# Expert blocks of 128 rows instead of 256, four to a slot, in batch groups of 5, 5, 4 and 2, with the sums at one pace

## The reference

```
x = layernorm(x + attention(x))          16 heads of 16 channels, rope, causal
x = layernorm(x + experts(x))

experts: probs = softmax(x @ gate_w.T)   32 experts
         top 8 of 32 per token, their weights made to sum to 1
         out = sum over the 8 experts e of
               w_e * ((u * silu(g)) @ down_w[e].T),   g, u = split(x @ gate_up_w[e].T)
```

## Time and profile before

| what | us |
|---|---|
| time of 3 runs: median (lowest, highest) | 2408.0 (2407.4, 2415.5) |
| span of the profiled execution | 2400.9 |
| between that span and the median (work around the span; the profiled execution's time is not listed apart) | 7.1 |
| PE busy | 2019.5 (84%) |
| DVE busy | 1642.8 (68%) |
| ACT busy | 1559.1 (65%) |
| POOL busy | 1124.8 (47%) |
| DMA engines, mean busy share, q1 (SP's queue) and q0 (POOL's) | 51.1% and 19.6% |

### The profile page before, as it was taken

How to read it: one execution, slowest core, us unless ns; L and a number is a source line. 1 busy time by engine, 2 the same in 40 slices (tenths; PEclk the granted TensorE clock), 3 DMA queues, 4 the chain that set the end, 5 groups by cost and what they waited for, 6 DMA issues and landing times.

```text
span 2400.9 us, 57843 instructions
## 1 busy us (share of the span) xinstructions
PE 2019.5 (84%) x18031; PEld 1445.3 (60%) x18031; DVE 1642.8 (68%) x3500; ACT 1559.1 (65%) x3163; POOL 1124.8 (47%) x1110
## 2 busy tenths in 40 slices
PE   4888888888888888888788899999899999998970
PEld 2444444454445444444446788788788788787760
DVE  4777777777776677777654555555577777777774
ACT  1566665666655555555456677777688788888870
POOL 1004345534553355544455005000677777777776
PEclk8899999999999899999999999999999999999995
DMA  5455667657766866557957669788999999999993
GB/s 169 129 168 187 190 213 241 199 181 218 247 209 200 281 217 221 183 173 229 318 174 256 213 205 342 254 270 279 316 353 333 317 339 322 327 336 320 318 302 116
DMA packets 330818, 591.91 MB, mean 247 GB/s; under 512 B 47168, under 2 KB 168416, under 8 KB 328416
## 3 DMA queue, kind: packets, MB, share of 16 engines
q1 hardware_dynamic: 251232, 400.17, 51.1%
q0 software_dynamic: 53760, 159.45, 19.6%
q10 hardware_dynamic: 25536, 28.58, 3.6%
HBM read 326.68 MB, written 299.50 MB: 261 GB/s over the span
## 4 chain that ended last, share of the span: by engine, by line
PE 37%; DMA 15%; DVE 15%; issue 11%; ACT 8%; POOL 6%; SPq 5%; ACTq 2%; DVEq 1%; POOLq 0%
POOL stacks L759 4%; DMA qk_parts<-pbuf 4%; DVE mn L1484 4%; PE ps L935 4%; PE ps L1008 4%; PE ps L989 3%; PE ps L876 3%; PE ps L991 3%; PE ps L990 3%; PE ps L923 3%; ACT work L1143 3%; PE ps L901 3%; SPq L591 2%; PE ps L825 2%; DMA stacks<-qk_parts 2%
## 5 line engine op out<-in xcount | busy, mean ns | idle before, releaser
L1143 ACT ACTIVATE pT<-ps 128x1024 f16<-128x1024 f16 (+4 forms) x1408 | 827.8, 601 | 428.6 <-PE ps L925 277.7
L743 POOL DMA_INDIRECT x_sorted<-xhl,idx x512 | 532.8, 1041 | 414.9 <-DVE xhl L1555 263.4
L759 POOL DMA_INDIRECT stacks<-y_sorted,idx x512 | 520.1, 1016 | 362.0 <-DMA y_sorted<-work 199.9
L1484 DVE TENSOR_REDUCE mn<-ps 128x1 f32<-128x512 f32 (+3 forms) x704 | 416.4, 633 | 93.7 <-PE ps L903 89.3
L989 PE MATMUL ps<-pT,gu_hi 128*128 128x256 f16 x1536 | 421.5, 274 | 18.4 <-issue 12.7
L990 PE MATMUL ps<-pT,gu_hi 128*128 128x256 f16 x1536 | 421.0, 274 | 0.0
L991 PE MATMUL ps<-pT,gu_lo 128*128 128x256 f16 x1536 | 420.8, 274 | 0.0
L923 PE MATMUL ps<-stacks 99*128 99x512 bf16 (+3 forms) x1024 | 310.7, 317 | 65.6 <-ACT pT L1143 44.7
L901 PE MATMUL ps<-stacks 96*128 96x512 bf16 (+3 forms) x1024 | 293.1, 319 | 58.7 <-DMA stacks<-qk_parts 31.6
L1051 PE MATMUL ps<-dn,vx 128*128 x768 | 210.1, 274 | 31.3 <-DVE work L1661 16.1
L1647 DVE TENSOR_TENSOR vx<-vx 128x512 f16<-128x512 f32 x192 | 132.4, 690 | 151.6 <-ACT vx L1143 137.2
(11 more groups left out here) (229 smaller groups left out, 3621.3 us busy)
## 6 DMA issues: line engine op xcount, KB each, us to landing
y_sorted<-work SPq DMA_DIRECT2D x288, 256.0 KB
stacks<-qk_parts SPq DMA_DIRECT2D x128, 384.0 KB, 5.1
x_sorted<-zeros_h SPq DMA_DIRECT2D x132, 288.0 KB
stacks<-x_sorted SPq DMA_DIRECT2D x88, 288.0 KB, 4.4
y_sorted<-yev SPq DMA_DIRECT2D x96, 256.0 KB
qk_parts<-pbuf SPq DMA_DIRECT2D x62, 384.0 KB
pT<-x_sorted SPq DMA_DIRECT2D x70, 288.0 KB
pbuf<-x_sorted SPq DMA_DIRECT2D x70, 288.0 KB
```

Source lines behind the costliest of these rows:

```text
L743: pool.indirect_dma_start(xsort[g][:, :], bass.IndirectOffsetOnAxis(ap=at, axis=0), xhl_rows[:, t, :], None).then_inc(s_scat, 16)
L759: pool.indirect_dma_start(yg[:, r, k, :].bitcast(I32), None, ysort[g][:, :], bass.IndirectOffsetOnAxis(ap=at, axis=0)).then_inc(s_yg[r], 16)
L1143: return nc.scalar.activation(o, i, f, **k)
L1484: V.tensor_reduce(mn[:, tt, h0:h0 + nh], ps[:, odd_bank("max", at, m), 0:nh * n].rearrange("p (a n) -> p a n", a=nh), axis=AX.X, op=ALU.ma ...
```

## The change

`BLK` becomes 128, and a slot holds four blocks, each with its own expert; what was a block of 256 rows is now a pair (`PAIR`), whose two halves are loaded, multiplied and stored apart. The worst case of blocks is (tokens x 8 / 128 + 32) per group, in slots of four 48 + 48 + 40 + 24 = 160. Groups are 5, 5, 4 and 2 batches. The register tables take 16 numbers at a time. The plan of sums gives a tile every 2.1 slots (`TILE_PACE` 21) once its group is ready: total 0 at slot 56, 47 totals (0 to 46) below slot 160, and 17 behind it. `bias` gives up its memory to share `rcb`'s, and the homes of the later part are taken in another order.

```diff
@@ -64,31 +64,29 @@
-BLK = 256
-GROUPS = ((0, 7), (7, 12), (12, 15), (15, 16))
+BLK, PAIR = 128, 256
+GROUPS = ((0, 5), (5, 10), (10, 14), (14, 16))
 NG = len(GROUPS)
...
 MB = GMAX * T // BLK
-NSLOT = [((hi - lo) * T * TOPK // BLK + E) // 2 for lo, hi in GROUPS]
+NSLOT = [((hi - lo) * T * TOPK // BLK + E) // 4 for lo, hi in GROUPS]
 SLOT0 = [sum(NSLOT[:g]) for g in range(NG + 1)]
...
 RW = 2 * C + 2 * E
-TILES = [(SLOT0[g + 1] + 8, SLOT0[g + 2] + 7) for g in range(NG - 1)] + [(S + 8, S + 12)]
-NK = TILES[-1][1]
 NXT = 4
...
 NYG = 3
-NREG = 8
+NREG, NTAIL = 16, 8
 RT = 11
...
 WT = 4
-TPARTS = [-(-2 * n // P) for n in NSLOT]
+TPARTS = [-(-4 * n // P) for n in NSLOT]
 TB = [0]
...
@@ -96,18 +94,21 @@
-    tiles_at = {}
-    for (lo, hi), (first, last) in zip(GROUPS, TILES):
-        tiles = list(range(lo * NT, hi * NT))
-        for k, q in enumerate(tiles):
-            tiles_at.setdefault(first + k * (last - first) // len(tiles), []).append(q)
+    tiles_at, at = {}, 0
+    for g, (lo, hi) in enumerate(GROUPS):
+        at = max(at, 10 * (SLOT0[g + 1] + 8))
+        for q in range(lo * NT, hi * NT):
+            tiles_at.setdefault(at // 10, []).append(q)
+            at += TILE_PACE
     return tiles_at
...
+TILE_PACE = 21
 TILES_AT = plan()
+FIRST_SUM, NK = min(TILES_AT), max(TILES_AT) + 1
 LATER = 2 * (SLOT0[1] - 12)
-EARLY_HOMES, LATE_HOMES = list(range(14)), list(range(10, 20))
+EARLY_HOMES, LATE_HOMES = list(range(14)), list(range(14, 20)) + list(range(10, 14))
 HOMES = [EARLY_HOMES[n % 14] if n < LATER else LATE_HOMES[(n - LATER) % 10] for n in range(2 * S)]
...
@@ -133,7 +134,7 @@
 def y_on_vector(n):
-    return n % 2 == 1 and n // 2 + LAG < TILES[0][0]
+    return n % 2 == 1 and n // 2 + LAG < FIRST_SUM
...
@@ -477,10 +478,10 @@
-                g = GROUP_OF[n // 2]
-                n -= (n - 2 * SLOT0[g]) % NREG
-                j = n - 2 * SLOT0[g]
-                count = min(NREG, 2 * NSLOT[g] - j)
+                g = GROUP_OF[n // 4]
+                n -= (n - 4 * SLOT0[g]) % NREG
+                j = n - 4 * SLOT0[g]
+                count = min(NREG, 4 * NSLOT[g] - j)
                 if j == 0:
...
@@ -593,15 +594,15 @@
             y_row = Table(sp, 2, [n - BLK for n in NROW])
-            tail_regs = [sp.alloc_register(f"tail_{k}") for k in range(NREG)]
+            tail_regs = [sp.alloc_register(f"tail_{k}") for k in range(NTAIL)]
...
                     wait(sp, s_tab, g + 1)
-                if e % NREG == 0:
-                    sp.load(tail_regs, ztab[0:1, g, e:e + NREG])
-                row = sp.snap(tail_regs[e % NREG], min_val=0, max_val=NROW[g] - BLK)
+                if e % NTAIL == 0:
+                    sp.load(tail_regs, ztab[0:1, g, e:e + NTAIL])
+                row = sp.snap(tail_regs[e % NTAIL], min_val=0, max_val=NROW[g] - BLK)
                 sp.dma_start(xsort[g][bass.ds(row, BLK), :].rearrange("(a b) c -> a (b c)", a=16),
...
@@ -625,14 +626,15 @@
                     wait(sp, s_yc[k % NYR], 2 * (k // NYR + 1))
-                src = xsort[g][bass.ds(x_row(n), BLK), :].rearrange("(p m) c -> p m c", m=2)
-                sp.dma_start(xrows[HOMES[n]], src).then_inc(s_xs[HOMES[n]], 16)
+                for m in range(2):
+                    sp.dma_start(xrows[HOMES[n]][:, m, :], xsort[g][bass.ds(x_row(2 * n + m), BLK), :]).then_inc(s_xs[HOMES[n]], 16)
...
                 wait(sp, s_yc[n % NYR], 2 * (n // NYR + 1))
-                dst = ysort[GROUP_OF[n // 2]][bass.ds(y_row(n), BLK), :].rearrange("(p m) c -> p m c", m=2)
-                sp.dma_start(dst, ysb[n % NYR].bitcast(I32)).then_inc(s_ys[n % NYR], 16)
+                for m in range(2):
+                    dst = ysort[GROUP_OF[n // 2]][bass.ds(y_row(2 * n + m), BLK), :]
+                    sp.dma_start(dst, ysb[n % NYR][:, m, :].bitcast(I32)).then_inc(s_ys[n % NYR], 16)
...
@@ -752,7 +754,7 @@
                     for k in range(NYR):
-                        wait(pool, s_ys[k], 16 * (2 * SLOT0[g + 1] // NYR))
+                        wait(pool, s_ys[k], 32 * (2 * SLOT0[g + 1] // NYR))
                 wait(pool, s_cmb, 7 * (q - NYG) + 3)
...
@@ -998,14 +1000,14 @@
                 k = BANK_X[n % 2]
-                wait(pe, s_xs[HOMES[n]], 16 * (len(uses_before(n)) + 1))
+                wait(pe, s_xs[HOMES[n]], 32 * (len(uses_before(n)) + 1))
                 if n < 2:
...
                     for m in range(2):
-                        last = nc.tensor.transpose(o[:, c * BLK + m * P:c * BLK + (m + 1) * P],
+                        last = nc.tensor.transpose(o[:, c * PAIR + m * P:c * PAIR + (m + 1) * P],
                                                    xnat[HOMES[n]][:, m, c * P:(c + 1) * P], identh[:, :])
...
@@ -1021,21 +1023,23 @@
                     n = 2 * s + a
-                    e, r = expert(n), n % NXT
+                    r = n % NXT
                     if m == 0:
                         wait(pe, s_xe, n + 1)
-
-                    def weights(w, kc):
-                        return w[:, bass.ds(e, 1), kc, m, :].rearrange("p o f -> p (o f)")
-                    last = hilo(ps[:, k, a * BLK:(a + 1) * BLK],
-                                [weights(gu_hi, kc) for kc in range(NC)], [weights(gu_lo, kc) for kc in range(NC)],
-                                [xT[:, r, kc, :] for kc in range(NC)], [xT[:, r, NC + kc, :] for kc in range(NC)])
+                    for b in range(2):
+                        e, rows = expert(2 * n + b), slice(b * BLK, (b + 1) * BLK)
+
+                        def weights(w, kc):
+                            return w[:, bass.ds(e, 1), kc, m, :].rearrange("p o f -> p (o f)")
+                        last = hilo(ps[:, k, a * PAIR + b * BLK:a * PAIR + (b + 1) * BLK],
+                                    [weights(gu_hi, kc) for kc in range(NC)], [weights(gu_lo, kc) for kc in range(NC)],
+                                    [xT[:, r, kc, rows] for kc in range(NC)], [xT[:, r, NC + kc, rows] for kc in range(NC)])
                 last.then_inc(done, 1)
...
                 n, r = 2 * s + a, s % 2
-                e, k = expert(n), y_bank(n)
+                k = y_bank(n)
                 wait(pe, s_h, s + 1)
...
@@ -1044,10 +1048,11 @@
                     wait(pe, s_yc[last_in_bank % NYR], 2 * (last_in_bank // NYR + 1))
-                d_hi, d_lo = (dn[:, bass.ds(e, 1), p, :].rearrange("p o c -> p (o c)") for p in range(2))
                 for m in range(2):
+                    e = expert(2 * n + m)
+                    d_hi, d_lo = (dn[:, bass.ds(e, 1), p, :].rearrange("p o c -> p (o c)") for p in range(2))
                     o = ps[:, k, m * C:(m + 1) * C]
-                    h_hi, h_lo = (h[:, r, a * BLK + m * P:a * BLK + (m + 1) * P] for h in (hh, hl))
+                    h_hi, h_lo = (h[:, r, a * PAIR + m * P:a * PAIR + (m + 1) * P] for h in (hh, hl))
                     mmul(o, h_hi, d_hi, start=True, stop=False)
...
@@ -1274,9 +1279,9 @@
                 wait(act, s_h, s - 1)
-                for a in range(2):
+                for a in range(4):
                     actv(hf[:, s % 2, a * BLK:(a + 1) * BLK], ps[:, BANK_G[s % 2], a * BLK:(a + 1) * BLK], ACT.Tanh,
-                         scale=mgh[:, bass.ds(expert(2 * s + a), 1)]).then_inc(s_th, 1)
+                         scale=mgh[:, bass.ds(expert(4 * s + a), 1)]).then_inc(s_th, 1)
...
@@ -1291,10 +1296,10 @@
                 else:
-                    wait(act, s_ys[n % NYR], 16 * (n // NYR))
+                    wait(act, s_ys[n % NYR], 32 * (n // NYR))
                 for m in range(2):
                     actv(ysb[n % NYR][:, m, :], ps[:, y_bank(n), m * C:(m + 1) * C], ACT.Copy,
-                         scale=xw[HOMES[n]][:, m, bass.ds(expert(n), 1)]).then_inc(s_yc[n % NYR], 1)
+                         scale=xw[HOMES[n]][:, m, bass.ds(expert(2 * n + m), 1)]).then_inc(s_yc[n % NYR], 1)
```

More of the change, by code:

```diff
@@ L252, in build @@
         bvc = sb("bvc", [P, NC])
-        bias = sb("bias", [P, C])
         ident = sb("ident", [P, P])
@@ L267, in build @@
         rcb = sb("rcb", [P, C])
+        bias = rcb
         mhalf = sb("mhalf", [P, NT])
@@ L310, in build @@
         ind = lg2[:, 1, :]
-        tab = sb("tab", [3, 2 * S], I32)
+        tab = sb("tab", [3, 4 * S], I32)
         ztab = sb("ztab", [1, NG, E], I32)
@@ L1597, in table_out @@
                 wait(dve, s_ttr, g + 1)
-                V.tensor_copy(tab[:, 2 * SLOT0[g]:2 * SLOT0[g + 1]], ps[0:3, odd_bank("table", GROUPS[g][1]), 0:2 * NSLOT[g]]).then_inc(s_tab, 1)
+                V.tensor_copy(tab[:, 4 * SLOT0[g]:4 * SLOT0[g + 1]], ps[0:3, odd_bank("table", GROUPS[g][1]), 0:4 * NSLOT[g]]).then_inc(s_tab, 1)
             def ln_add(b, v):
@@ L1631, in gated @@
             def gated(s):
-                wait(dve, s_th, 2 * s + 2)
+                wait(dve, s_th, 4 * s + 4)
                 V.scalar_tensor_tensor(out=hf[:, s % 2, :], in0=hf[:, s % 2, :], scalar=1.0, in1=ps[:, BANK_G[s % 2], :],
@@ L1658, in rows_copy @@
                 else:
```

(4 more changed lines are left out.)

## The result

The changed kernel takes 2539.0 us (median of 4 runs, 2538.3 to 2546.5), the kernel before beside it 2407.7: ratio **1.0579** (95% interval 1.0548 to 1.0610), 131 us slower. The forecast was 2388, its range ended at 2450. The profiled span is 2536.5 us, 135.6 longer than before.

The account below looks back on a forecast made before the run. PE's register instructions were to set the pace: 5.24 + 0.37 table load + 0.27 waits = 5.88 us a slot; 1282.5 + 159 x 5.88 + 163 = 2380 us span, plus 7.1 gives 2388 us, range 2330 to 2450.

Parts of the forecast that it names:

- The bound moves to instructions, not columns: PE in a slot: register and other sequencer instructions, 5.24 us, exceed the array's 4.90 and set the pace.
- rival D: PE's array: 128-column matmuls that load their own weights take over 0.056 us; time 2480, chance 0.05.
- PE's floor of 5.61: PE per slot: 5.24 us of sequencer instructions plus 0.37 for its table load.
- SP at 5.3 a slot: SP: eight issues of 0.525 us, table loads and the sums' transfers take 5.3 us a slot, hidden behind PE's 5.6.
- rival C: SP issues in order, so transfers come late and PE waits each slot; 6.27 us a slot, time 2450, chance 0.31.
- The excess: 0.27 kept of 0.63: Waits per slot beyond the array's 4.83 us were 0.63; 0.27 of it was taken to stay above PE's new floor.
- Table loads as a term of PE alone: PE's load of 16 numbers every fourth slot adds 0.37 us a slot; ACT's and SP's loads stay below PE's floor.
- The sequencer is ahead, which now it never is: PE's sequencer, as the bound, never runs ahead, so short waits aren't caught up; all 0.63 us a slot could stay.
- the first of the two signs of being wrong: PE's gate_or_up matmuls going on 0.056 us apart over several groups while register instructions keep their spacing would refute the forecast.
- The end: After the last slot, 17 tiles instead of 7 remain: 163 us against 76.8 before.
- Attention at 0: Register tables built at other batches during attention: cost put at 0, between -5 and +5 us.
- Rival B: PE's register instructions run beside the array's queue at no new cost; slot stays 5.45 us, time 2319, chance 0.12.

Follow-up runs that it names:

- e9: The changed kernel with PE taking a fixed expert's weights, so no register instructions or table load on PE; 2470.7 us, ratio 1.0295.
- e5: The changed kernel with gate and up in matmuls of 256 columns, both blocks of a pair using the first block's expert; 2491.5 us, ratio 1.0372.
- e7: The changed kernel with each pair loaded from fixed sorted rows by one SP transfer (the fixed load); 2486.0 us, ratio 1.0372.
- e8: The changed kernel with pairs loaded from fixed rows by one transfer and gate and up in matmuls of 256 columns; 2409.9 us, ratio 1.0040.
- e6: The changed kernel with ACT and DVE loading their table numbers only once, using other experts' scales; 2502.3 us, ratio 1.0428.
- e14: The changed kernel with 256-column gate and up, one fixed-row transfer per pair, and table loads ahead of the waits; 2352.8 us, ratio 0.9811.
- g1: The kernel before with table loads issued ahead of the waits, results unchanged; 2386.5 us, ratio 0.9947.

## Why the prediction was wrong, point by point

- **The bound moves to instructions, not columns: right in direction.** Eight transposes take 0.45, gate products are 0.056 apart where they aren't starved; rival D is out. But PE's sequencer was not the only one that it moved to.
- **PE's floor of 5.61: a little low.** The instructions came as counted (44.6 for 44.8 a slot), 0.118 each where nothing stops them (gate groups 0.237 apart from 2139.36 to 2140.07). The table load, every fourth slot, has a median of 1.25, a mean of 1.37 in 1900 to 2200 us and 0.36 behind it, so about 0.43 a slot for 0.37. That gives 5.7 (the 5.9 in the expectations above takes 0.12 and 0.48). This is the smaller part.
- **SP at 5.3 a slot, "hidden behind 5.6": wrong, and the step that failed.** The 0.525 of the earlier trace rows is the distance of issues that all take 0.34 to 0.36 us. Among the sums an issue takes 0.43 on average, 29 of 404 in 300 us over 0.6, and with what stands around it a transfer costs 0.64; 8.8 of them (the sums' included) are 5.6, and table loads make it 6.1. So SP's floor is above PE's, and it is the one that stands when PE's register work is taken away (e9, 6.2 to 6.4). It was to be had before: 275 issues took 112.6 us there, 0.41 each, and SP was taken for 3.4 of 5.45 us a slot, not "under half". With 6.1, rival C would have been the likeliest case.
- **The excess: 0.27 kept of 0.63, wrong in kind.** I treated the waits as one amount laid on top of one floor. In fact PE (5.7) and SP (6.1) are both nearly full and the measured excess over the higher floor is 0.6 (0.4 in 1950 to 2250 us). That each waits for the other by way of ACT, and neither has the slack to catch up, is argued from e5, e7 and e8, not measured by itself.
- **Rival C: nearer than the forecast, but its sign didn't show.** It named SP, but at a price of 2450, at most 2475, that came from adding the whole 0.63 to PE's 5.61. In the changed kernel PE's waits for `x_sorted` in 1950 to 2250 us are 12.0 us (14.5 before), those for "issue" 15.6 (7.5 before); the waits for transfers grow only when PE is relieved (e9).
- **Table loads as a term of PE alone: wrong, in the whole stage.** The earlier trace rows showed one holding the chain. With 16 numbers PE's, ACT's and DVE's come one after another in the same slot: four slots of 5.0, 5.6, 6.2 and 10.3 (slots 0 to 47) where it was 4.8, 5.1, 5.6 and 6.9. Among the sums it is 5.7, 5.2, 6.3 and 9.8 (before: 4.6, 6.4, 3.5 and 7.3). Early, this and PE's register work are what holds the slots, since the fixed load gives nothing there. e6 gives 1.7 us of an early table slot back.
- **"The sequencer is ahead, which now it never is": wrong.** The eight transposes of a turn need no register instruction, and meanwhile PE's sequencer works ahead. Seven gate groups then follow with 0.056 a matmul, and the eighth comes late (timeline of PE, changed kernel):

```profile
2141.56 0.22 PE L991 MATMUL ps<-pT,gu_hi 128*128 128x128 f16 x1
...
2142.67 0.22 PE L993 MATMUL ps<-pT,gu_lo 128*128 128x128 f16 x1
2142.78 0.23 PE L991 MATMUL ps<-pT,gu_hi 128*128 128x128 f16 x1
```

  Its register instructions of line 991 are 0.25 apart over these groups (seven from 2141.2 to 2142.7). That is the first of the two signs of being wrong that the prediction named. It lasts as long as the lead does; over a whole slot the instructions still count, as e5 shows early on.
- **ACT: right.** Four tanh took 1.02 us (1.03 forecast), and no run shows ACT's work, apart from its table loads, as a bound.
- **DMA engines: right that they had room.** 0.85 busy in the late stretch; among the sums they no longer set the pace.
- **The end: right.** 168.3 us, 163 forecast. It is also the largest single difference to the kernel before, +91.5 us.
- **Attention at 0:** the first slot came 15.1 us later, but 3 to 10 later in e5 to e14, which have the same attention stage, and 6.6 later in g1, which is the kernel before in that stage. It varies between runs; how much of it belongs to the change isn't shown.
- **Rival B** (register instructions cost nothing) is out: without them undisturbed early slots are 4.8, with them 5.1 to 5.6.

## What to carry to other kernels

When a change halves a tile, count for every queue the instructions that don't shrink with it, SP's above all, and price each at its average start-to-start time in the stretch in question, not at the shortest spacing. The sum of an engine's waits in a stretch is the budget that such a change may spend: SP had 115 us of 300, and 2.7 us a slot more left 18. Two queues that were both nearly full cost more here than the fuller one (6.73 for 6.1 and 5.7), and relieving one showed only part of what relieving both gave. Where several engines fetch the same numbers at the same step, fetch them ahead of the waits.

## What was not expected of the hardware

A table load's cost goes with its numbers: 1.25 us on PE for 16 against 0.87 for 8, and with the instructions behind it (0.19 and 0.17 for 16) and the engines in series, two loads of 8 were no dearer than one of 16 (26.4 for 27.1 us in four slots). Issues by SP, mostly 0.35 us, at times take 1.1 to 1.5 us for the same kind of transfer. And PE's granted clock fell from 1.00 to 0.97 in the late stretch (and from 0.99 to 0.97 in 1300 to 1640 us). Behind a wait of 2.17 us in e5 PE's matmuls run at half speed: the granted clock is 1.00 in 2136 to 2140 us, 0.56 in 2140 to 2142 and 0.50 in 2142 to 2146, and matmuls of 256 columns start 0.21 us apart where the earlier trace rows have 0.109 (timeline of PE):

```profile
2140.30 1.03 PE L1010 MATMUL ps<-identh,xin 128*128 128x128 f16 x8 [2.17 <-DMA xin<-x_sorted]
2142.70 0.37 PE L991 MATMUL ps<-pT,gu_hi 128*128 128x256 f16 x1 [1.36 <-issue]
2142.86 0.42 PE L992 MATMUL ps<-pT,gu_hi 128*128 128x256 f16 x1
2143.07 0.42 PE L993 MATMUL ps<-pT,gu_lo 128*128 128x256 f16 x1
```

A mean of 0.97 is some 6% of the time at 1.2 GHz, so an estimate of at most 0.2 us a slot in the changed kernel. It looks like an effect of the waits that adds to them; no run parts it from them.
